# VectorE's order inside the batch loop of a fused attention and expert kernel

## What is computed

```python
x = x + attn(cond(x, cond_512, ...), Wq, Wk, Wv, Wpost)   # attn returns X + softmax(Q K / 8) V Wpost
# cond2, per token: kx = modulated_linear(x); kx -> [16 heads, 8]
scores = einsum('bnhd,bnjd->bnhj', kx, kx) / sqrt(8)
A = softmax(scores, axis=-1)
out = modulated_linear(einsum('bnhj,bnjd->bnhd', A, kx))
# ffn: logits = out @ gate_w.T, top 2 of 8 experts, those over capacity left out
x = x + sum_e comb[:, e] * (relu(out @ W1[e] + b1[e]) @ W2[e] + b2[e])
```

## Time and profile before

| what | value |
|---|---|
| median of 3 runs | 538.81 us (537.04 to 538.97) |
| the profiled execution, its own time | 537.42 us |
| its span | 535.5 us |
| TensorE matmul busy | 504.0 us, 94% of the span |
| VectorE busy | 419.3 us, 78% |
| ScalarE busy | 372.5 us, 70% |
| GpSimd busy | 323.4 us, 60% |
| mean granted TensorE clock | 0.996 |

### The profile page before, as it was taken

How to read it: one execution, slowest core, us unless ns; L and a number is a source line. 1 busy time by engine, 2 the same in 40 slices (tenths; PEclk the granted TensorE clock), 3 DMA queues, 4 the chain that set the end, 5 groups by cost and what they waited for, 6 DMA issues and landing times.

```text
span 535.5 us, 12870 instructions
## 1 busy us (share of the span) xinstructions
PE 504.0 (94%) x3896; PEld 356.4 (67%) x3896; DVE 419.3 (78%) x715; ACT 372.5 (70%) x851; POOL 323.4 (60%) x328
## 2 busy tenths in 40 slices
PE   7899999999999999999999999999999979969997
PEld 7766666666666666666666666666666756656665
DVE  4234788888888888888888888888888877754766
ACT  3467777777777777777777777777777537657783
POOL 1103677777777777777777777777777657203860
PEclk9999999999999999999999999999999999999999
DMA  6500000000000000000000000000000000000004
GB/s 228 135 1 2 2 1 2 1 0 0 0 0 0 0 0 0 0 0 0 0 0 0 0 0 0 0 0 0 0 0 1 1 2 0 2 0 2 0 11 148
DMA packets 9364, 7.19 MB, mean 13 GB/s; under 512 B 1088, under 2 KB 8832, under 8 KB 9216
## 3 DMA queue, kind: packets, MB, share of 16 engines
q1 hardware_dynamic: 9344, 6.94, 4.3%
HBM read 4.84 MB, written 2.10 MB: 13 GB/s over the span
## 4 chain that ended last, share of the span: by engine, by line
PE 52%; issue 16%; ACT 13%; DVE 12%; POOL 2%; ACTq 1%; DMA 1%; SPq 1%; DVEq 0%; POOLq 0%
PE misc L704 6%; PE bank_a L697 6%; PE bank_t L679 5%; PE bank_d L712 5%; PE bank_t L947 4%; PE bank_s L664 4%; ACT prob L1001 4%; PE bank_d L689 4%; DVE mix_lo L447 3%; DVE attT L308 3%; PE bank_t L674 2%; PE bank_s L955 2%; PE bank_d L955 2%; DVE h_den L437 2%; PE misc L834 2%
## 5 line engine op out<-in xcount | busy, mean ns | idle before, releaser
L1362 POOL TENSOR_TENSOR pair<-kx 128x1152 f32<-128x1152 f32 x32 | 82.7, 2584 | 115.2 <-DVE shifted L418 93.2
L300 DVE TENSOR_REDUCE row_max<-bank_s 128x4 bf16<-128x512 f32 x128 | 89.3, 697 | 43.0 <-PE bank_s L664 38.1
L1347 POOL TENSOR_TENSOR mix_hi<-mix_hi 128x512 f32<-128x512 f32 (+2 forms) x96 | 104.8, 1092 | 7.5
L712 PE MATMUL bank_d<-attT,wpost_sb 128*128 128x128 f32 x512 | 70.7, 282 | 1.6 <-DVE attT L308 0.6
L1001 ACT ACTIVATE prob<-bank_t 128x512 f32<-128x512 f32 x128 | 68.8, 593 | 3.6 <-PE bank_t L679 3.6
L704 PE MATMUL misc<-yT,wq_sb 128*128 128x128 f32 x512 | 68.2, 277 | 0.0
L712 PEld LDWEIGHTS bank_d<-attT,wpost_sb 128*128 128x128 f32 x512 | 62.0, 192 | 7.0 <-DVE attT L308 6.8
L679 PE MATMUL bank_t<-qT,kT 64*128 64x256 f32 x512 | 65.7, 376 | 0.0
L308 DVE TENSOR_TENSOR attT<-bank_a,inv_den 128x512 f32<-128x512 f32 x64 | 43.8, 686 | 25.1 <-ACT inv_den L1001 14.4
L704 PEld LDWEIGHTS misc<-yT,wq_sb 128*128 128x128 f32 x512 | 62.9, 194 | 0.7
L1340 POOL TENSOR_TENSOR mix_hi<-weight,kx 128x1024 f32<-128x1024 f32 x32 | 63.0, 1970 | 0.0
(11 more groups left out here) (183 smaller groups left out, 943.7 us busy)
## 6 DMA issues: line engine op xcount, KB each, us to landing
out<-acc_all SPq DMA_DIRECT2D x8, 256.0 KB, 2.3
x_all<-in_xT SPq DMA_DIRECT2D x1, 1024.0 KB, 9.8
w_sb<-in_w SPq DMA_DIRECT2D x2, 512.0 KB
x_all<-in_xT SPq DMA_DIRECT2D x1, 768.0 KB, 7.5
wq_sb<-in_wq SPq DMA_DIRECT2D x1, 512.0 KB, 6.1
wpost_sb<-in_wpost SPq DMA_DIRECT2D x1, 512.0 KB, 9.7
x_all<-in_xT SPq DMA_DIRECT2D x1, 256.0 KB, 3.2
b_rows<-in_b SPq DMA_DIRECT2D x16, 4.0 KB
```

The costliest lines, as they stand in the source:

```text
L300: V.tensor_reduce(bass.AP(row_max, first_w * (P + 1) + HPG * p, [[HPG * P, P], [P + 1, 2], [KEY, 2], [1, 1]]), bank_s[:, :, :].rearrange(" ...
L712: last = mm(bank_d[:, 0, :], wpost_sb[:, k, :], attT[:, k, :], start=(k == 0), stop=(k == CHUNKS - 1))
L1347: G.tensor_tensor(mix_hi[:, jd, 0:r, :], mix_hi[:, jd, 0:r, :], mix_hi[:, jd, r:2 * r, :], ALU.add).then_inc(s_hi, 1)
L1362: G.tensor_tensor(pair[:, :, :], bass.AP(kx2, jc * 2 * P, [[4 * P, P], [0, SHIFTS], [1, P]]), bass.AP(kx2, jc * 2 * P, [[4 * P, P], [MD, S ...
```

## The change

Only the order of VectorE's calls in `loop_slot` changes. The same instructions with the same operands are issued, and the other engines' streams are untouched. `normalise(c, 1)` goes in front of `heads_max(s, 3)`. `head_scores` and `attended` go in front of `weight_sums` and `weighted_rows`, with `head_scores` first. `row_sum` follows directly on `weighted_rows`.

```diff
                 def loop_slot():
+                    if C:
+                        normalise(c, 1)
                     if B:
                         heads_max(s, 3)
+                    head_scores()
                     if C:
-                        normalise(c, 1)
+                        attended()
                     if D:
                         weight_sums()
                         weighted_rows()
-                    if C:
-                        attended()
-                    head_scores()
-                    if D:
                         row_sum()
                     if A:
                         heads_max(a, 0)
```

## The result

The changed kernel took 534.94 us (median of 10 runs, 532.48 to 536.18) against 537.98 us (10 runs) of the kernel before. The ratio is 0.9937, with a 95% interval of 0.9916 to 0.9958. By this ratio the changed kernel takes 3.4 us less; the two medians differ by 3.0 us. The forecast was 533.5 us, with a range of 531 to 536.

A forecast was written before the change was run, and what follows sets the result against it. A slot was taken as bound by TensorE's work and waits or a ring through VectorE, after the change by a ring of 12.73 us. 3.8 us from 27 turns with 0.9 at the edges made 4.7, forecast 533.5 us, range 531 to 536.

The forecast's parts named there:

- the idle time: VectorE in front of `heads_max(s, 3)`: 0.56 us a slot waiting for its bank, to be filled by `normalise(c, 1)`.
- bound by `posts`: VectorE's `attended`, now held by TensorE's `posts`, would start at 204.74, 1.17 us earlier than 205.91.
- the add of 512: GpSimd's first add, 1.26 us alone: `weighted_rows` would wait 0.81 us for it and end 1.08 us after it.
- a new wait of 12.5 us for `row_max`: TensorE before `scores(a, 1)`: about 0.5 us of idle a slot, some 10 to 15 us in all.
- The ring: Repeating chain, `heads_max(a, 0)` through GpSimd's add, `weighted_rows`, `row_sum`: 8.45, 1.26, 1.08, 0.10, 1.84; sum 12.73 us against 12.88.
- 27 x 0.14: Loop gain: 27 turns between slots 3 and 30, each 0.14 us shorter, 3.8 us.
- The edges: Slots 1, 2 and 31, bound by TensorE: the 0.9 us that `posts` waited for `attT` is gained in full.
- the sum: Whole kernel: 3.8 us from the loop with 0.9 us from slots 1, 2 and 31, 4.7 us gained.
- the two engines share: Rival, 10%: `weighted_rows` runs beside GpSimd's add in 1.16 us; slot 12.22 us, kernel some 519 to 520 us.
- the order gives nothing: Rival, 18%: the wait for GpSimd costs 0.1 us more; ring 12.83 to 12.88 us, kernel 536 to 538.5 us.
- VectorE loses the hand-over: Rival, 12%, slower: GpSimd's second add goes ahead of waiting `weighted_rows`; ring 13.54 us, kernel about 555 us.
- The rule beside it: VectorE instructions with two SBUF inputs and GpSimd's exclude each other for a whole instruction; by it the forecast is 533.5 us.

The follow-up runs named there:

- e1: Kernel before with only `normalise(c, 1)` moved in front of `heads_max(s, 3)`: 536.42 us, ratio 0.9976.
- e2: Changed kernel with `normalise(c, 1)` moved back behind `heads_max(s, 3)`, the rest in the new order: 534.97 us, ratio 0.9957.
- e3: Changed kernel with GpSimd's first add covering 128 elements in place of 512, three quarters of that sum left out: 515.50 us, ratio 0.9604.
- e4: Changed kernel with GpSimd's two copies of the scores between its product and its three adds, nothing left out: 517.42 us, ratio 0.9628.
- e7: Changed kernel with GpSimd's add of 512 split into two adds of 256, no wait between them: 517.41 us, ratio 0.9628.
- e6: Changed kernel with `weight_sums` moved between `head_scores` and `attended` on VectorE, GpSimd untouched: 518.69 us, ratio 0.9660.
- e8: Changed kernel with GpSimd's add of 512 split into two adds of 256 and a semaphore wait between them: 516.38 us, ratio 0.9619.

## Why the prediction was right

**The mechanism held at each step.** `normalise` fitted into the idle time. `attended` became bound by `posts`. `weighted_rows` met the add of 512 in place of the product, the add of 256 was stretched in its place, and TensorE got a new wait of 12.5 us for `row_max`, foreseen as 10 to 15. e1 and e2 put the loop's gain into the second part of the change; e3 shows that the add under way is what holds it back.

**Two terms were mis-sized.** The ring was put at 12.73 us and measured 12.78. Its terms in the slot shown are 8.43 + 1.27 + 1.09 + 0.10 + 1.89 = 12.78: the other four stand within 0.02 us of the forecast, but `row_sum` needs 1.89 to the next start and not 1.84. I took its 1.92 us from the old place; the row of it directly behind `mix_lo` showed 1.96 and was at hand. And the step "27 x 0.14" used 0.14 for what became 0.10, and one turn too many: from slot 29 to slot 30 the distance is 12.40 us before and 12.41 after, so the ring gained in 26 turns only. That makes 2.6 us in place of 3.8. The edges had been put at 0.9 us; 3.4 less 2.6 leaves 0.8, nearly all of it in slots 1 and 2 (0.39 us each). So the sum was 4.7 us for a measured 3.4, and the forecast of 533.5 was too low by about as much, 1.4 us; its range held the measured time. That the profiled execution took 532.53 us, beside the 532.7 that the sum gave for it, is luck: 3.1 us of its lead lie in front of the first `row_max`, where no call was moved.

**The rivals.** That the two engines share falls: when the add is in the way, `mix_lo` takes 1.9 us, and 1.2 when it is not (e3, e4). Its price, a kernel at 519 to 520 us if the wait were gone, was close: e4 has 517.4, with 12.16 us a slot where the prediction had 12.22. That the order gives nothing falls by the interval and by the slot: the wait costs 1.09 and 0.10 in the loop too, and the slot is 12.78 us and not 12.83 or more. That VectorE loses the hand-over falls too: in the changed kernel `mix_lo` took no more than 1.93 us in any slot of the hardware loop, and in e7 VectorE got in even without a gap.

**The rule beside it.** The Trainium skill (SBUF — State Buffer, "SBUF: two separate sides") has the loser fully block until the other's instruction ends. The runs agree: 1.21 us or 2.33 us for one instruction, by who was issued first.

## What to carry to other kernels

When two engines exclude each other, a long instruction of the less busy one can set the time of the busiest. Look at whose end a stretched instruction follows, and by how much; then cut that other instruction in two, put a short one in its place, or be issued first. A reorder that closes a wait pays only as far as the next one: here a slot could fall from 12.88 to 12.16 us, 0.10 of these 0.72 us were gained, and the rest came back only when GpSimd's add got out of the way (e4, e6, e7, e8). TensorE then stood idle for less than 1 us of the 330 from 60 to 390 us, in e4 not at all.

## What the runs showed that I had not expected

A `weighted_rows` that waited for GpSimd ends 1.07 to 1.09 us after GpSimd's instruction, some 0.12 us less than the 1.21 that it takes in the loop unhindered. VectorE gets in between two GpSimd instructions even where the trace shows no gap between them (e7: the second starts at 196.68, the first ends at 196.73), if it was issued before the second. And a margin of under 0.1 us in the order of issue decided 1.1 us in single slots of e6, in a program whose order never changes.
